# The two diagonal row-maximum pieces of a head group issued as one interleaved pair

## The reference, cut to what matters

```
attn = jnp.einsum('bqhd,bkhd->bhqk', q, k) * scale
attn = jnp.where(causal, attn, jnp.float32(-jnp.inf))
attn = jax.nn.softmax(attn, axis=-1)
out  = jnp.einsum('bhqk,bkhd->bqhd', attn, v)
```

## Time and profile before

| what | value |
|---|---|
| time, median of 3 runs | 8470.32 us (8468.65 to 8478.94) |
| span of the profiled execution, first to last instruction | 8471.3 us |
| PE busy | 7608.0 us (90%) |
| DVE busy | 7340.3 us (87%) |
| ACT busy | 5072.8 us (60%) |
| POOL busy | 3704.5 us (44%) |
| first attention: prologue, then iterations | 203.89 to 270.2, to 1864.2 us |
| second attention: prologue, then iterations | 6325.9 to 6392.2, to 7995.4 us |

### The profile page before, as it was taken

One profiled execution on the slowest core, in us unless ns is written; L12 is line 12 of the kernel. 1 busy time (PEld: TensorE's weight loads), 2 busy tenths in 40 slices (PEclk: granted clock), 3 DMA queues, 4 the chain that ended last, 5 costly groups with the idle time before them and its releaser, 6 DMA issues. The chain is left out here.

```text
span 8471.3 us, 131822 instructions
## 1 busy us (share of the span) xinstructions
PE 7608.0 (90%) x38817; PEld 3068.7 (36%) x38818; DVE 7340.3 (87%) x10750; ACT 5072.8 (60%) x7665; POOL 3704.5 (44%) x1825
## 2 busy tenths in 40 slices
PE   6999999989987888888888888888889999999899
PEld 3333333325542333333333333333453333333355
DVE  6988888858877999999999999999658888888588
ACT  3577777762255666666665556556316777777622
POOL 0010011100016999999999999999400000110000
PEclk9899999989998999999999999999988999999999
DMA  6001101112262222222233333333561001010121
GB/s 177 18 19 20 19 19 19 20 37 70 67 232 91 85 83 83 84 83 83 83 98 103 100 100 100 101 103 97 164 181 18 19 19 19 19 22 18 36 78 61
DMA packets 531283, 603.88 MB, mean 71 GB/s; under 512 B 195488, under 2 KB 344736, under 8 KB 526560
## 3 DMA queue, kind: packets, MB, share of 16 engines
q1 hardware_dynamic: 526048, 562.63, 22.4%
q0 software_dynamic: 4608, 33.56, 2.0%
HBM read 397.75 MB, written 163.69 MB: 66 GB/s over the span
## 5 line engine op out<-in xcount | busy, mean ns | idle before, releaser
L833 DVE TENSOR_REDUCE ffn_att_mx<-psum 128x1 f32<-128x512 f32 (+3 forms) x4608 | 2728.0, 654 | 367.8 <-PE psum L674 209.2
L794 ACT ACTIVATE ffn_att_e<-psum,unscale 128x1024 f32<-128x1024 f32 (+3 forms) x2560 | 2376.5, 985 | 766.3 <-PE psum L739 760.3
L1707 POOL TENSOR_TENSOR scan_h<-scan_h,scan_cs 128x1024 f32<-128x1024 f32 x1024 | 2412.4, 2449 | 203.8 <-ACT scan_state L1878 198.0
L1788 PE MATMUL psum<-scan_h,ident 128*128 128x512 f32 x4096 | 1977.7, 624 | 158.9 <-POOL scan_h L1707 157.6
L2022 DVE TENSOR_TENSOR_SCAN scan_h<-psum,scan_state,scan_db 128x512 f32<-128x512 f32 x1408 | 1684.6, 1261 | 10.5 <-ACT psum L1920 10.5
L641 POOL TENSOR_SCALAR_AFFINE_SELECT ffn_att_e<-ffn_att_e 128x512 f32<-128x512 f32 x512 | 324.6, 634 | 3023.9 <-ACT ffn_att_e L794 3023.9
L674 PE MATMUL psum<-ffn_att_k,ffn_att_q 48*128 48x512 f16 (+3 forms) x5120 | 1438.8, 367 | 175.4 <-DMA ffn_att_v<-v 55.8
L1788 PEld LDWEIGHTS psum<-scan_h,ident 128*128 128x128 f32 x4096 | 777.7, 198 | 1321.1 <-issue 894.5
L705 PE MATMUL psum<-ffn_att_e,ffn_att_v 128*32 128x512 f32 (+3 forms) x10240 | 1240.4, 557 | 7.8 <-ACT ffn_att_o L809 2.4
L1920 ACT ACTIVATE psum<-scan_dt,scan_anr 128x512 f32<-128x512 f32 x1024 | 698.2, 682 | 460.2 <-DVE scan_h L2022 459.4
L674 PEld LDWEIGHTS psum<-ffn_att_k,ffn_att_q 48*128 48x128 f16 x5120 | 394.8, 94 | 1559.4 <-DVE ffn_att_mx L833 1260.7
(11 more groups left out here) (256 smaller groups left out, 7118.0 us busy)
## 6 DMA issues: line engine op xcount, KB each, us to landing
scan_cs<-scan_bcd SPq DMA_DIRECT2D x520, 256.0 KB, 3.2
scan_bs<-scan_bcd SPq DMA_DIRECT2D x162, 256.0 KB, 3.4
scan_win<-xp SPq DMA_DIRECT2D x34, 1036.0 KB, 7.0
scan_dt<-scan_sp POOLq DMA_DIRECT2D x32, 1024.0 KB, 7.0
mamba_out_ffn_in_ys<-yz SPq DMA_DIRECT2D x18, 1024.0 KB, 7.6
scan_yi<-y SPq DMA_DIRECT2D x17, 1024.0 KB, 6.7
ffn_att_q<-q_parts SPq DMA_DIRECT2D x128, 128.0 KB, 2.8
ao<-ffn_att_on SPq DMA_DIRECT2D x128, 128.0 KB
```

The costliest lines, as they stand in the source:

```text
L794: nc.scalar.activation(E[:, s % PB, 2 * hp:2 * hp + 2, off:CH], psum[:, 2 * hp:2 * hp + 2, off:CH], ACT.Exp, scale=unscale[:, 0:1]).then_i ...
L833: nc.vector.reduce_max(mx[:, hh * 2 + pairs[0]:hh * 2 + pairs[1], i // HALF, i % HALF, c // TT], psum[:, turn, 0:(pairs[1] - pairs[0]) * w ...
L1707: nc.gpsimd.tensor_tensor(hh, hh, cs[:, n % NCS, :].unsqueeze(1).to_broadcast([P, 2, CH]), ALU.mult).then_inc(hc_ready, 1)
L1788: ins = nc.tensor.matmul(psum[:, m, :], ident[:, :], h[n % NH][:, m, :], start=False, stop=n == DS - 1)
```

## The change

`maximum` keeps the off-diagonal pieces. A new function `diagonal_pair` does the two partners of a diagonal couple together: for each head, the product of the first half and the product of the second half, then first mask of the one and of the other, second mask of the one and of the other. The counts, shapes and banks of the products are the same. The signal to VectorE (`m_ps`) is still sent for each piece, now by the last mask of each. The wait for the second partner's bank (`free(n + 1)`) stands directly behind the first partner's first product.

```
-                        for z in range(2 * is_diag):
-                            ins = nc.tensor.matmul(psum[:, turn, (j + 1) * w - P:(j + 1) * w], pick[rows_at, 1 - hh + z, :],
-                                                   mask[rows_at, 1 - hh + z, :], start=False, stop=z == 1, tile_position=(hh * ROWS, 0))
+                                               start=True, stop=True, tile_position=(hh * ROWS, 0))
                     ins.then_inc(m_ps, 1)
 
+                def diagonal_pair(par, n, turns, free):
+
+                    q, k = Q[par], K[par]
+                    i, c, w, pairs, _ = pieces[n]
+                    for j, pair in enumerate(range(*pairs)):
+                        for hh in range(2):
+                            if j == 0:
+                                free(n + hh)
+                            at = slice(hh * ROWS, hh * ROWS + PARTS)
+                            nc.tensor.matmul(psum[:, turns[hh], j * w:(j + 1) * w],
+                                             q[at, i // HALF, pair, i % HALF * P:(i % HALF + 1) * P], k[at, c * P:c * P + w],
+                                             start=True, stop=False, tile_position=(hh * ROWS, 0))
+                        for z in range(2):
+                            for hh in range(2):
+                                at = slice(hh * ROWS, (hh + 1) * ROWS)
+                                ins = nc.tensor.matmul(psum[:, turns[hh], (j + 1) * w - P:(j + 1) * w], pick[at, 1 - hh + z, :],
+                                                       mask[at, 1 - hh + z, :], start=False, stop=z == 1, tile_position=(hh * ROWS, 0))
+                                if z == 1 and pair == pairs[1] - 1:
+                                    ins.then_inc(m_ps, 1)
+
                 def maxima(when, it, par, todo):
 
                     for kind, n in todo:
+                        i, c, _, _, hh = pieces[n]
                         if (kind, n) == ("head", 0):
                             pe.wait_ge(loaded[(par + 1) % NBUF], LOADS * ((it + 1) // NBUF + 1))
+                        at = par if kind == "tail" else (par + 1) % NBUF
+                        if c + TT > i:
+                            if hh == 0:
+                                diagonal_pair(at, n, [turn_bank(when, (kind, n + z)) for z in range(2)],
+                                              lambda z: bank_is_free(when, it, (kind, z)))
+                            continue
                         bank_is_free(when, it, (kind, n))
-                        maximum(par if kind == "tail" else (par + 1) % NBUF, n, turn_bank(when, (kind, n)))
+                        maximum(at, n, turn_bank(when, (kind, n)))
```

More of the change, by code:

```diff
@@ L670, in maximum @@
                     i, c, w, pairs, hh = pieces[n]
-                    at, rows_at = slice(hh * ROWS, hh * ROWS + PARTS), slice(hh * ROWS, (hh + 1) * ROWS)
-                    is_diag = c + TT > i
+                    at = slice(hh * ROWS, hh * ROWS + PARTS)
                     for j, pair in enumerate(range(*pairs)):
@@ L675, in maximum @@
                                                q[at, i // HALF, pair, i % HALF * P:(i % HALF + 1) * P], k[at, c * P:c * P + w],
-                                               start=True, stop=not is_diag, tile_position=(hh * ROWS, 0))
-                        for z in range(2 * is_diag):
-                            ins = nc.tensor.matmul(psum[:, turn, (j + 1) * w - P:(j + 1) * w], pick[rows_at, 1 - hh + z, :],
-                                                   mask[rows_at, 1 - hh + z, :], start=False, stop=z == 1, tile_position=(hh * ROWS, 0))
+                                               start=True, stop=True, tile_position=(hh * ROWS, 0))
@@ L716, in _, with first_is_free @@
                 pe.wait_ge(loaded[0], LOADS)
-                for n in range(T):
+                def first_is_free(n):
                     if n >= 3:
                         pe.wait_ge(m_red, n - 2)
-                    maximum(0, n, 5 + n % 3)
+                for n in range(T):
+                    i, c, _, _, hh = pieces[n]
+                    if c + TT <= i:
+                        first_is_free(n)
+                        maximum(0, n, 5 + n % 3)
+                    elif hh == 0:
+                        diagonal_pair(0, n, [5 + (n + z) % 3 for z in range(2)], first_is_free)
                     if n == NP0 + 1:
```

## The result

The changed kernel takes 8481.32 us (median of 20 runs, 8465.94 to 8493.55) against 8469.47 us before (20 runs). The ratio is 1.0014, 95% interval 1.0008 to 1.0020: 7 to 17 us slower, by the middle 12 us. I had forecast 8496 us, 26 us slower. That the loss would be more than 0.2% had a chance of 0.66 and did not come true; it is 0.14%.

A forecast was written before the change was run, and what follows sets the result against it. In iterations VectorE and TensorE take turns as bound; in prologues VectorE is the path. Terms -5 + 16 + 15 = +26 us gave 8496 us, forecast 8487 to 8507, eight in ten between 8480 and 8515.

The forecast's parts named there:

- TensorE gets little back: Iterations: only two-headed couples with a free bank gain, -0.18 us in each of 30 executions, -5 us in all.
- The term for couple 110: Iterations, pieces 110 and 111 (w = 256): 0.18 us comes free, so piece 112 comes earlier.
- The first result comes late: All couples: the first piece is ready only with its partner; prologues pay +16 us, uncovered places in iterations +15 us.
- The term of +16 us: Two prologues: late first pieces cost 8.2 us in each, uncovered since VectorE is busy there without a pause.
- The start: Prologue, couples 2 and 4: piece 2 comes 0.79 us late and piece 4 with it; 0.9 us for both.
- The iterations, +15 us less the gain of 5: Iterations: uncovered lateness at pieces 30, 70, 126 and 142 costs +15 us; TensorE's regained time gives -5 us.
- piece 126: Iterations: its reduce comes 0.16 us late in 32 executions and makes TensorE late too, with a small pause behind it.
- the lateness of piece 4: Iterations: piece 4 comes 0.43 us late, covered by VectorE's 0.80 us idle time ahead of piece 6.
- The iterations hide all lateness: Rival: VectorE's pauses in the iterations take up all lateness, leaving +16 - 5 = +11, 8481 us; chance 0.23.
- Strict program order of the products: Rival: halves run in program order, so the pause ahead of diagonal pieces shrinks; -104 us at most, 8366 us; chance 0.05.
- The clock rival: Iterations: idle TensorE makes the 1.2 GHz stretches grow by a third, costing about 16 us, 8512 us; chance 0.08.
- Busy times stay: Sign expected in the profile after: the engines' busy times do not change; no size given.

The follow-up runs named there:

- the wait alone: Kernel before with its product order kept, only the second partner's bank wait moved ahead of the first partner's first product: 8496.0 us, ratio 1.0037.
- seven banks: Changed kernel with prologue pieces going round seven banks instead of three, the last nine round three again: 8467.26 against 8468.78 us before, ratio 0.9996.
- the masks-by-half run: Changed kernel with each head's four masks ordered first half's two, then second half's two: 8470.19 us, ratio 1.0006 to the kernel before.
- the last version: Changed kernel with prologue pieces round seven banks and the first half's masks ahead of the second's: 8458.95 against 8468.78 us before, ratio 0.9991.

## Why the prediction was right, and where its sizes were wrong

- **TensorE gets little back.** Right. Couples with one head per half ran side by side before, and two-headed ones gain only where the bank is free. The term for couple 110 was 0.18 us; measured 0.185. Couple 2 gave nothing.
- **The first result comes late; the prologue pays it in full.** Right in mechanism (the wait alone reproduces it, seven banks remove it) and in the place. The term of +16 us measured 12.2. Mis-sized was "the end of the *second* piece's masks" as the time at which the first is ready: the first is signalled when the partner's first mask has ended, one mask earlier. At the half clock a mask is 0.107 us. In the profile after the couples of w = 384 behind another of 384 are late by 0.33 us (I had 0.43), w = 512 by 0.30 (0.40), w = 256 by 0.50 (0.60). That is 0.1 us in each of 17 couples, 1.7 of the 2.1 us that a prologue's sum of 8.2 was too high. The start cost 0.68 and not 0.9 us. And after the couples of w = 128 the next two intervals are 0.11 us shorter than before, so 0.19 us stays of each (I had 0.40): VectorE had a little slack there, which I had taken for none.
- **The iterations, +15 us less the gain of 5.** This is where the sum went wrong. By profile the net is +0.09 us an iteration, +3 us in all, and the run with the iterations alone finds +1 us (-7 to +8). Two steps of it failed. The same mask: 30 and 70 are late by 0.11, not 0.16 us, and 142 by 0.03, not 0.08. And piece 126, carried on with 0.16 us, is hidden. I took its cover for "a small pause", but two reduces in a row overlap by 0.08 us, so a VectorE that shows a pause of 0.04 us has 0.12 us to give; the interval 127 to 128 gave back 0.12. The rest was nearly as said: the lateness of piece 4 (I had 0.43, measured 0.38) is taken by the pause ahead of 6, piece 58 by the pause ahead of 64, the others by their steps.
- **The rivals.** "The iterations hide all lateness" was given 8481 us and a chance of 0.23. That is the measured time, and partly by luck, for it comes about by a different split: the iterations hide nearly all, and the prologues are 4 us cheaper, with the gain at 110 in balance against pieces 30 and 70. Strict program order of the products, which the Trainium skill's page "TensorE: Matmul & The Clock Gate" (Part 3, "The mechanism") states for starts and ends, holds here for the signals, by the masks-by-half run, and not for the starts: the products of pieces 28 and 29 both start by 609.99, the first mask, which stands between them in program order, at 610.15. The clock rival shows nothing: 0.97 in the stretch of rows 2, as before. In working it out I made a slip: a mean of 0.97 between full and half speed is 6% of the time at the half clock, not 3%. "Busy times stay" was not right either: VectorE's in the prologue rose by 1.05 us, TensorE's in the stretch of rows 2 fell by 20.

What stays open: whether the gain of the last version is more than its countable 1 to 3 us. Single profiles say nothing about 10 us here. The iterations of the kernel before and of the one with only the prologues changed are the same code, yet last 3197 and 3186 us in their traces, while the medians of all intervals between pieces agree to 0.05 us, except the one between 135 and 136 (0.06). That one is decided by the clock: in all the traces it is 1.11 to 1.12 us where it falls at the full clock and 1.87 to 2.85 us where a stretch at 1.2 GHz touches it (21 of 28 times before, 20 with only the prologues changed). The medians of the other intervals and the prologues are free of this.

## What to carry to other kernels

Two streams of work that wait for different buffers shouldn't be zipped unless both buffers are free by then: the first otherwise waits for the buffer of the second, and its consumer with it. Here the seven banks took that cost away. Before alternating products over TensorE's halves, look in the timeline whether they already run together, and who is the path. Where VectorE was the path, in the prologue, what TensorE saved was worth nothing, and a result that came later than VectorE's next start cost its lateness in full. To see what a reorder does, compare the new ready time with the consumer's *start* in the old trace, for each case.

## What the runs showed of the hardware

- Products on the two halves of the rows start out of program order: in rows 3 the second half's product starts with the first's, ahead of two masks. Their completion signals keep program order: after the change the first half's last mask ends at 618.93 and VectorE starts at 619.09, 0.04 us behind the end of the partner's earlier mask. The increments themselves, in 12 couples of a prologue, come 0.23 to 0.34 us behind the piece's own last product and 0.021 or 0.022 us behind the end of the other half's product ahead of it.
- A reduce that finds its input ready starts 0.08 us before the one ahead has ended (0.465 us from start to start at 0.55 us each). A pause in the profile is therefore 0.08 us smaller than the slack.
- The granted clock stayed at 0.50, 1.2 GHz, through the whole prologue in every one of the kernels, with TensorE's busy time there at 58 to 65 us of 66 to 75, and a mask took 0.107 us from start to start instead of 0.06.
